# First layer of a two-layer graph attention kernel: the order of TensorE's work in a tile step, and the step in which a tile is summed

## The reference

```python
# layer 0: typed attention
Q, K, V = (enh @ Wq + bq), (enh @ Wk + bk), (enh @ Wv + bv)      # each N x 4 x 64
mod_k  = K[src] + 0.2 * rel_w[edge_type][:, None, :]
scores = einsum('ehd,ehd->eh', Q[dst], mod_k) / 8
w      = softmax of scores over the edges of one dst
agg    = segment_sum(w[:, :, None] * V[src], dst)
x      = layernorm(x + layernorm(agg @ Wo + bo + x) * gamma + beta)
# layer 1: plain attention (GAT) with a self loop for each node
xp     = (x @ W).reshape(N, 4, 64)
alpha  = leaky_relu(a_src[src] + a_dst[dst]);  softmax over dst;  agg = sum of w * xp[src]
x      = layernorm(x + elu(agg + bias))
```

## Time and profile before

| what | us |
|---|---|
| median of 3 runs | 4633.29 (4626.58 to 4635.58) |
| the profiled execution: its own time | 4628.61 |
| its span, first to last instruction | 4627.2 |
| tables and projection of the nodes | the first 350 or so |
| first layer (`attend_typed`), first L851 to last L962 | 359.1 to 2464.7 |
| second layer, gathers of rows to the end | 2500 or so to 4627 |

### The profile page before, as it was taken

The page is one execution under the profiler, slowest core; times in us unless marked ns, Lnnn a source line. Parts: engine busy times, 40 slices in busy tenths (PEclk is TensorE's granted clock), DMA queues, the critical chain, the costliest instruction groups (busy, mean ns, idle before and its releaser), DMA issues. The chain is left out here.

```text
span 4627.2 us, 149696 instructions
## 1 busy us (share of the span) xinstructions
PE 3929.3 (85%) x42462; PEld 2568.6 (56%) x42462; DVE 3415.2 (74%) x11602; ACT 2795.2 (60%) x7985; POOL 3143.2 (68%) x3229
## 2 busy tenths in 40 slices
PE   6988999999999999999996778778877877777874
PEld 4655555555555555555554556555555555555553
DVE  3235788777777778777775578888778778787777
ACT  2324555555555555555553677777777777777775
POOL 1217777777777777777772777777777777777773
PEclk9998999999999999999997677777778777787777
DMA  6878888888888888888884777777777777777774
GB/s 207 282 236 246 259 259 259 257 259 259 259 255 260 258 260 258 257 258 261 259 256 120 187 206 206 207 204 205 207 207 205 205 204 205 205 208 209 203 206 131
DMA packets 820558, 1052.06 MB, mean 227 GB/s; under 512 B 458633, under 2 KB 632338, under 8 KB 820464
## 3 DMA queue, kind: packets, MB, share of 16 engines
q0 software_dynamic: 225072, 726.83, 53.9%
q1 hardware_dynamic: 594078, 323.35, 27.0%
q10 hardware_dynamic: 1314, 0.99, 0.1%
HBM read 915.79 MB, written 133.39 MB: 227 GB/s over the span
## 5 line engine op out<-in xcount | busy, mean ns | idle before, releaser
L1286 POOL DMA_INDIRECT plain_rows<-xp,plain_index x1563 | 1559.8, 998 | 554.9 <-issue 440.8
L765 POOL DMA_INDIRECT typed_rows<-kv,typed_index x1563 | 1511.2, 967 | 626.2 <-issue 414.3
L1391 PE MATMUL plain_p_o<-plain_rows,plain_weight_t 128*64 128x130 f32 (+1 forms) x8336 | 856.5, 348 | 44.0 <-DVE plain_weight_t L1417 43.3
L1158 ACT ACTIVATE typed_weight<-typed_weight,typed_col 128x416 f32<-128x416 f32 x521 | 334.6, 642 | 855.0 <-DVE typed_col L991 809.5
L1378 PE MATMUL plain_p_s<-all_cst,plain_rows 128*128 128x128 f32 (+1 forms) x2084 | 455.0, 318 | 368.2 <-DMA plain_rows<-xp,plain_index 365.9
L1391 PEld LDWEIGHTS plain_p_o<-plain_rows,plain_weight_t 128*64 128x64 f32 (+1 forms) x8336 | 570.2, 169 | 203.8 <-issue 128.5
L1378 PEld LDWEIGHTS plain_p_s<-all_cst,plain_rows 128*128 128x128 f32 (+1 forms) x2084 | 335.2, 174 | 522.6 <-issue 504.8
L989 DVE CUSTOM_DVE_ANT_0 typed_weight<-typed_p_s,typed_far 128x416 f32<-128x416 f32 x521 | 305.1, 586 | 371.5 <-PE typed_p_s L874 347.8
L874 PE MATMUL typed_p_s<-typed_kt,typed_q 64*32 64x416 f32 x4168 | 472.4, 521 | 103.4 <-issue 73.0
L1424 DVE CUSTOM_DVE_ANT_0 plain_alpha<-plain_alpha,plain_far 128x416 f32<-128x416 f32 x521 | 310.0, 595 | 311.4 <-ACT plain_alpha L1540 296.4
L962 DVE TENSOR_TENSOR typed_kt<-typed_p_kt,typed_rel 128x768 f32<-128x768 f32 x521 | 494.7, 950 | 3.7 <-PE typed_p_kt L851 3.4
(11 more groups left out here) (190 smaller groups left out, 6303.5 us busy)
## 6 DMA issues: line engine op xcount, KB each, us to landing
typed_match<-match SPq DMA_DIRECT2D x131, 208.0 KB
plain_match<-match SPq DMA_DIRECT2D x131, 208.0 KB
agg<-qkv_zero SPq DMA_DIRECT2D x98, 264.0 KB
typed_agg<-agg SPq DMA_DIRECT2D x98, 264.0 KB
plain_agg<-agg SPq DMA_DIRECT2D x98, 264.0 KB
kv<-qkv_kv SPq DMA_DIRECT2D x98, 258.0 KB
typed_kinds<-match SPq DMA_DIRECT2D x131, 192.0 KB
typed_rows<-kv,typed_index POOLq DMA_INDIRECT x1563
```

Of the source, the lines that this page charges most:

```text
L765: pool.indirect_dma_start(rows[:, r, j, :], None, k.kv, bass.IndirectOffsetOnAxis(ap=index[:, g, at:at + 1], axis=0)).then_inc(rows_in[r], 16)
L1158: act.activation(weight[:, c], weight[:, c], ACT.Exp, bias=col[:, t.slot(4), LOW:LOW + 1]).then_inc(exp_done, 1)
L1286: pool.indirect_dma_start(rows[:, r, j, :], None, k.xp, bass.IndirectOffsetOnAxis(ap=index[:, g, at:at + 1], axis=0)).then_inc(rows_in[r], 16)
L1391: last = pe.matmul(p_o[at:at + HC, t.slot(2), 0:2 * V], weight_t[0:e, t.slot(2), j * P + at:j * P + at + HC], val[:, 2 * V * g:2 * V * g + ...
```

## The change

It calls PE's parts in another order and moves `aggregate` one tile forward, so that tile n-5 is turned and summed in the same step n; ACT's parts and the lag of the write to DRAM follow. PE's order becomes `turn_weights(n-5)`, `score(n-3)`, `relate(n)`, `aggregate(n-5)`, `arrive(n-1)`. DVE's order is not touched. No instruction is added or removed in the steady steps.

```diff
 def attend_typed(k):
-    R, M, KEY, SCORE, TURN_LAG, LAG = 8, 4, 1, 3, 5, 6
+    R, M, KEY, SCORE, TURN_LAG, LAG = 8, 4, 1, 3, 5, 5
...
-            interleave(sp, FIRST, TilePart(8, put_out), TilePart(0, fetch), BlockPart(0, 0, load), BlockPart(6, 10, store))
+            interleave(sp, FIRST, TilePart(7, put_out), TilePart(0, fetch), BlockPart(0, 0, load), BlockPart(6, 10, store))
...
             def step(t, copied=None):
-                for part in (TilePart(TURN_LAG, turn_weights), TilePart(LAG, lambda b: aggregate(b, copied)), TilePart(SCORE, score),
-                             TilePart(0, relate), TilePart(KEY, arrive)):
+                for part in (TilePart(TURN_LAG, turn_weights), TilePart(SCORE, score), TilePart(0, relate),
+                             TilePart(LAG, lambda b: aggregate(b, copied)), TilePart(KEY, arrive)):
                     part.at(t)
...
-            interleave(act, FIRST, BlockPart(2, 1, copy_message), TilePart(TURN_LAG + 1, copy_weights), TilePart(LAG + 1, put), TilePart(SCORE + 1, weigh), TilePart(1, copy_relations), TilePart(SCORE, set_apart),
+            interleave(act, FIRST, BlockPart(2, 1, copy_message), TilePart(TURN_LAG + 1, copy_weights), TilePart(1, copy_relations), TilePart(SCORE + 1, weigh), TilePart(LAG + 1, put), TilePart(SCORE, set_apart),
                        BlockPart(4, 9, copy_x1), BlockPart(4, 10, copy_row), BlockPart(5, 8, keep_x1))
```

## The result

| | before | after |
|---|---|---|
| median, us | 4629.93 (4 runs, 4624.7 to 4635.58) | 4891.17 (4 runs, 4889.35 to 4893.27) |
| span of the profiled execution | 4627.2 | 4891.4 |
| first layer, start of the last L962 | 2464.7 | 2722.0 |

The ratio is 1.0564, 95% interval [1.0546, 1.0582]: slower by 5.6%. Of the 264.2 us by which the profiled span grew, 257.3 lie in the first layer (2464.7 to 2722.0). The other 7 stand behind it, where the code is the same; they are 0.15% of the whole, and a single profile of each can't say more of them. On two other occasions the kernel before took about 6140 us and not 4630; the runs of experiments 1 to 4 and the first of 6 fell there, and of them only ratios to the kernel before, run beside them, and undisturbed single steps are read.

What follows compares the result with a forecast made beforehand. PE was taken as the bound, its sums covering the key addition's latency within 0.02 us. Waits, updates, fourth tiles and late weights summed to 4.545 us per tile, +257 us on 4628.6, forecast 4890, range 4800 to 4980.

Steps and rivals of the forecast that it cites:

- The exposed addition: Between arrival and next score on PE: only the turning covers the key addition, PE waits 0.71 us, steps take 4.06.
- my point: On PE, the moment it alone would be ready for the next score, 3.35 us after a score's start.
- The unseen pair: On PE, sums to arrival isn't in the trace; taken as 0.73 us, the longer bound adding 0.12 to every step.
- the sums behind an update: On PE, sums starting 4.7 us after the latest arrival began, taking 0.72 us with no wait in them.
- Late weights: DVE's weight copy behind `join` and `normalize` makes PE's sums wait 0.44 and 0.27 us, each 3 times in 16.
- What goes away: Today's waits at PE's score for DVE's longer chain, up to 0.71 us, vanish; they are inside today's 4.046.
- fourth tiles: On DVE, L961 goes ahead of the key addition and is always on the path: +0.14 us in 4 of 16 steps.
- plain steps: PE's score-to-score steps without an update: 4.06 us after the change, in 13 of 16; PE's own step was 3.34.
- The sum: First layer: 72.7 us for 16 tiles, 4.545 per tile against 4.046, +257 us over 521 tiles.
- The clock: PE's clock in the first layer stays full (1.00), with PE busy about 83% of a plain step.
- Rival D: Slower, and PE's clock falls: half the time at half clock adds 545 us, giving 5435; chance 0.06.
- Rival B: Faster: relief from DVE's chain in block steps, 3.79 us per tile, 133 us less, 4500; chance 0.05.

Runs made afterwards that it cites:

- experiments 1 to 4: Kernels run where the kernel before took about 6140 us: sums of previous tile, sums behind arrival, ACT's order alone, half key addition; ratios 0.9869, 0.99, 1.0042, 0.9853.
- the first of 6: First run of the order with arrival ahead of score and key addition ahead of bounding: 6033.62 us against 6143.17 for the kernel before, ratio 0.9814.
- experiment 4: Changed kernel with half of the key addition left out (keys of two heads): 6047.92 and 6055.6 us, ratios 0.9853 and 0.9856 to the kernel before.
- 1: Changed kernel's PE order, but summing the tile before (LAG 6): 6062.89 and 6071.2 us, ratios 0.9869 and 0.9877 to the kernel before.
- experiment 2: Changed kernel, LAG 5 kept, with the sums moved behind the arrival: 6068.82 and 6096.45 us, ratios 0.99 and 0.9916 to the kernel before.
- experiment 6: Changed kernel with PE's arrival ahead of the score and DVE's key addition ahead of the bounding: 6033.62 and 4548.47 us, ratios 0.9814 and 0.9823 to the kernel before.
- experiment 5: Key addition cut in two halves, each releasing two heads: changed kernel 4981.89 us, kernel before 4730.73, order with sums behind the arrival 4738.82; kernel before unsplit 4627.64.
- the kernels with the split: Three kernels with the key addition in two halves: changed kernel 4981.89 us, kernel before 4730.73, sums behind the arrival 4738.82.
- the kernel before with the split: Kernel before, its key addition cut in two halves that each release two heads: 4730.73 us against 4627.64, ratio 1.0217.

## Why the prediction was right

The forecast was 4890 us, in 4800 to 4980, and 4891.17 was measured. By its own steps:

- **The exposed addition.** Said: arrival to addition 0.91, to the score 1.05, a wait of 0.71, a step of 4.06. The trace has 0.91, 1.06 and 4.07. PE's idle time is listed as 0.66, since the turning's last transposes end 0.06 behind my point. That the wait is the addition's length is shown by experiment 4, that it hangs on the place of the sums by 1 and 5.
- **The unseen pair.** Sums to arrival were put at 0.73 by their distance to the score; the rows have 0.73 (615.02 to 615.75). For the other new neighbours, in experiment 2, that would have failed: its shortest step is 3.48 and not 3.34. (The prediction sets the sums behind an update 4.7 us after the arrival began; by its rows it is 3.75. Nothing hangs on it.)
- **Late weights.** Said: 0.44 behind `join` and 0.27 behind `normalize`. The mechanism is there: 30.6 us of PE's 2000 are listed as idle ahead of L889 for L970. Its size was put too high. I average the steps from 400 to 2400, score to score, by their place among 16: behind each `join` 0.39 to 0.40 are lost, behind two of the three `normalize` 0.19, and behind the third nothing, since there the score has slipped by itself. That is 1.56 us in 16 tiles, not 2.13. This is the step of the prediction that was mis-sized.
- **What goes away.** DVE's chain no longer holds the score: DVE waits for PE at L962 for 162 us.
- **A term that the sum lacks.** The prediction takes 1.05 us from the addition to a waiting score. In three of 16 steps it is more, 1.29, 1.29 and 1.20, together 0.62 us. Timeline of DVE and PE in the third:

```profile
639.70 0.96 DVE L962 TENSOR_TENSOR typed_kt<-typed_p_kt,typed_rel 128x768 f32<-128x768 f32 x1 [0.67 <-PE typed_p_kt L851]
...
640.89 0.90 PE L874 MATMUL typed_p_s<-typed_kt,typed_q 64*32 64x416 f32 x8 [0.80 <-DVE typed_kt L962]
```

  In these steps the trace has two or three register and semaphore instructions of PE's own sequencer (of lines 866, 868 and 869) between the end of the addition and the score; in the other waiting steps it has none there. So fourth tiles take 4.19 in two cases of four and 4.44 in the other two. The kernel before has it too (1.30, 1.30 and 1.19 at the same places); its 4.046 per tile contains this, while the sum for the changed kernel was built from plain steps.
- **The sum.** Said 4.545 us per tile, measured 4.542; said +257 us for the layer, measured 257.3. That the terms of the mechanism are right is no luck, but agreement to 0.003 us is: the 16 average steps add up to 72.8 us, the predicted ones to 72.7, and in that 0.57 too much for late weights and the missing 0.62 cancel. So do the 7 us behind the layer, which were put at nothing, and the median, put at 4.7 us above the profiled execution and measured 1.6 under it (4891.17 against 4892.81).
- **The clock.** 1.00, as reckoned. The rule on short idles between groups of matmuls, of the Trainium skill (TensorE: Matmul & The Clock Gate, "A second HAM failure mode: psum-queue depth-cycling"), did not come true here: 0.66 us of idle time in every 4.06 left the clock where it was. Rival D fell with it.
- **Rival B** had its mechanism right and its place wrong. The waits that DVE's chain makes in the kernel before are worth having: experiment 6 takes them and wins 84 us. The change takes them too and pays more than twice their price.

## What to carry to other kernels

Ask of each instruction that is moved what latency it was covering, not only what it waits for: here 0.73 us of sums stood between a transfer to another engine and the instruction that needed its return, cover and latency met within 0.02 us, and moving the cover made it a wait in 13 of 16 steps. The right move was the opposite one: send the work to the other engine as early as possible and put everything else between. And a wait put between products that run side by side on TensorE cost the whole group's time again here: 0.82 us for two of four.

## What the runs showed of the hardware that was not expected

- **A pair of heads takes as long as four.** 0.82 us against 0.84 for products at different places of the array (experiment 5).
- **The order of neighbours matters on PE alone.** With the sums behind the transposes the shortest step is 3.48 us, with the other orders 3.33 or 3.34, though the instructions are the same; of the kernels with the split it is 3.48 against 3.33. The sums start 0.80 us after the first transpose, where the turning starts 0.71 after it, and the turning stands 0.58 ahead of the score and not 0.53 ahead of the sums. Nothing waits there that the profile names.
- **Semaphore and register instructions of PE can stand on the path.** They add 0.14 to 0.24 us to a wait for another engine in three of 16 steps, in both kernels (see the missing term above).
- **One DVE instruction and one wait of PE more per tile of the first layer slowed the second.** In the kernel before with the split, the second layer's sums run from 2589.3 to 4696.9, 2107.6 us, against 2554.2 to 4586.8, 2032.6 us, in the kernel before, with the same code. The waits of that layer (2640 to 4540) show it as pauses of DVE that no releaser explains (us in all, times, the longest), and the page's list of queues has more fetched instructions; in the kernel before the same queue moved 80 packets, 0.66 MB:

```profile
DVE plain_weight_t L1421 <- issue: 121.9, 25, 6.2
```

```profile
q14 instruction: 217, 1.77, 0.1%
```

  25 pauses of up to 6.2 us. The 75 us are most of the 110 by which the profiled span grew (4627.2 to 4737.3). All three kernels with the split have 215 or 217 packets on that queue, all eleven others 80 or 81. That the fetches are what the pauses wait for is likely by this, but not shown; what in the program's layout sets them off wasn't tried.
- **The kernel before took 4630 or 6140 us**, on different occasions and at least once on a chip of the same number; the kernels of the 6140 occasions have pauses inside unbroken runs of PE's instructions. Their queue of instructions moved 80 packets, so it is another thing than the point above. The cause stays open.
